# VectorE and ScalarE work through a block of linear attention in another order

## What is computed

```python
x = x + linear_attention(layernorm(x))     # x: 4 sequences, 2048 tokens, 256 features; 16 heads of 16
x = x + moe(layernorm(x))                  # 8192 tokens, 8 experts of 512, 2 for each token

# linear_attention: q = elu(x@Wq+bq)+1, k = elu(x@Wk+bk)+1, v = x@Wv+bv; per head and token i:
s = s + outer(k_i, v_i);  z = z + k_i
y_i = (q_i @ s) / (q_i @ z + 1e-6)         # then y @ Wo + bo

# moe: router logits, the two best experts, softmax over the two
out_t = sum over the two experts e of prob_e * (gelu(x_t@w1[e].T+b1[e]) @ w2[e].T + b2[e])
```

## Time and profile before

| | us |
|---|---|
| median of 3 runs (lowest, highest) | 1023.68 (1023.34, 1023.85) |
| the profiled execution, its own time | 1024.11 |
| its span in the trace | 1022.3 |
| PE busy | 917.8 (90%) |
| DVE busy | 754.4 (74%) |
| ACT busy | 681.3 (67%) |
| POOL busy | 621.1 (61%) |

### The profile page before, as it was taken

How to read it: one execution, slowest core, us unless ns; L and a number is a source line. 1 busy time by engine, 2 the same in 40 slices (tenths; PEclk the granted TensorE clock), 3 DMA queues, 4 the chain that set the end, 5 groups by cost and what they waited for, 6 DMA issues and landing times. The chain is left out here.

```text
span 1022.3 us, 33747 instructions
## 1 busy us (share of the span) xinstructions
PE 917.8 (90%) x10786; PEld 745.5 (73%) x10787; DVE 754.4 (74%) x2281; ACT 681.3 (67%) x1296; POOL 621.1 (61%) x564
## 2 busy tenths in 40 slices
PE   6799899899989999999987659899999999999995
PEld 3577677767777677767766338678999999999994
DVE  6689788988888888888887556456666666666663
ACT  8778888888878988888875315445555555555552
POOL 2135776777677767786673644447655565656565
PEclk9999999999999999999999769999999999999998
DMA  7626744554555354644441743435655656555554
GB/s 195 199 79 204 244 129 150 153 175 125 152 150 176 125 154 142 186 132 144 141 150 47 279 137 70 68 61 96 93 97 89 98 89 98 89 98 88 95 91 51
DMA packets 102584, 131.32 MB, mean 128 GB/s; under 512 B 15056, under 2 KB 89296, under 8 KB 101648
## 3 DMA queue, kind: packets, MB, share of 16 engines
q1 hardware_dynamic: 74336, 92.54, 32.2%
q0 software_dynamic: 25680, 35.01, 18.7%
q10 hardware_dynamic: 2464, 2.38, 0.7%
HBM read 64.29 MB, written 65.60 MB: 127 GB/s over the span
## 5 line engine op out<-in xcount | busy, mean ns | idle before, releaser
L1906 POOL DMA_INDIRECT out<-yt,to_token x135 | 216.7, 1605 | 176.6 <-DVE yt L1744 80.2
L1274 DVE SCALAR_TENSOR_TENSOR ahl<-pS,ahl 128x512 f16<-128x512 f32 x240 | 161.2, 682 | 42.4 <-ACT ahl L984 38.4
L984 ACT ACTIVATE ahl<-pS 128x512 f16<-128x512 f32 x240 | 142.2, 599 | 49.5 <-PE pS L654 32.2
L1789 POOL DMA_INDIRECT expert_in<-xn,cur x128 | 131.6, 1028 | 30.2 <-issue 26.0
L1196 ACT ACTIVATE g<-pS,b1s 128x256 f32<-128x256 f32 (+1 forms) x140 | 57.3, 462 | 94.6 <-PE pS L564 94.6
L564 PE MATMUL pS<-gT,w1s 128*128 128x256 f16 (+1 forms) x840 | 97.3, 272 | 4.3 <-DVE gT L1703 3.5
L564 PE MATMUL pF<-w2s,ghl 128*128 x816 | 95.6, 273 | 2.4 <-issue 1.5
L1710 DVE TENSOR_TENSOR ghl<-g,ghl 128x1024 f16<-128x1024 f32 (+1 forms) x68 | 83.0, 1221 | 19.4 <-ACT ghl L1221 12.6
L564 PE MATMUL pU<-w2s,ghl 128*128 x804 | 94.2, 273 | 1.9 <-issue 1.5
L564 PE MATMUL pF<-xT,was 128*128 128x512 f16 x384 | 92.8, 379 | 3.0 <-DVE xT L1279 2.9
L1783 POOL TENSOR_TENSOR state<-state,ut 128x272 f32<-128x272 f32 x64 | 49.9, 780 | 73.4 <-DVE ut L1314 72.5
(11 more groups left out here) (226 smaller groups left out, 2170.2 us busy)
## 6 DMA issues: line engine op xcount, KB each, us to landing
xg<-expert_in SPq DMA_DIRECT2D x64, 260.0 KB
qk_parts<-qkhl SPq DMA_DIRECT2D x64, 256.0 KB, 2.1
qst<-qk_parts SPq DMA_DIRECT2D x192, 64.0 KB
kst<-qk_parts SPq DMA_DIRECT2D x96, 128.0 KB
xs<-x SPq DMA_DIRECT2D x16, 512.0 KB
out<-x SPq DMA_DIRECT2D x16, 512.0 KB
w1raw<-w SPq DMA_DIRECT2D x16, 256.0 KB
w2raw<-w SPq DMA_DIRECT2D x4, 1024.0 KB, 7.2
```

Of the source, the lines that this page charges most:

```text
L984: nc.scalar.activation(ahl[:, b % 2, 0, n * 4 * C:(n + 1) * 4 * C], score_bank(fr, n)[:], ACT.Relu).then_inc(sc_hi, 1)
L1274: V.scalar_tensor_tensor(ahl[:, b % 2, 1, cols], score_bank(fr, n)[:], 0.0, ahl[:, b % 2, 0, cols], ALU.max, ALU.subtract).then_inc(sc_lo, 1)
L1789: G.indirect_dma_start(xg_dram, bass.IndirectOffsetOnAxis(ap=cur[:, qp, 2 * b + t:2 * b + t + 1], axis=0), xn2[:, qp, b], None).then_inc(s ...
L1906: G.indirect_dma_start(out, bass.IndirectOffsetOnAxis(ap=to_token[:, c % 2, s:s + 1], axis=0), yt[:, c % 2, s], None, compute_op=ALU.add). ...
```

## The change

Nothing is computed differently. VectorE's `router` is cut in two: `router_logits` (two instructions) stays where it was, the rest (maxima, indices, counts) moves behind `attention(3)`, `state_part(3)` and `logit_part(2)`. `norm2_shift` moves from ahead of `attention(0)` to behind `score_lo(1, 2)`; `out_lo(0)` comes ahead of the first statistics; `attention(1)` comes ahead of `residual(0)`; `score_lo(2, 3)` comes ahead of `norm1_shift` and `w1_low`. On ScalarE, `score_hi(2, 0)` comes ahead of `qk_high(2)` and `norm2_apply(0)`, and `out_hi(1)` and `score_hi(2, 2)` ahead of `norm2_apply(1)`. TensorE keeps its order and gets one wait: `out_transpose(s, 1)` also waits until `residual(s, 0)` has written x1.

```diff
--- before.py
+++ after.py
@@ -691,6 +691,8 @@
                     if g:
 
                         pe.wait_ge(lga_done, g)
+                        if b == 1:
+                            pe.wait_ge(x1_done, g)
                     for k in range(KC):
                         mm = nc.tensor.transpose(pA[:, k * C:(k + 1) * C], at[:, k * P:(k + 1) * P], ident)
                     mm.then_inc(aT_ps, 1)
@@ -1113,11 +1115,12 @@
                     score_hi(1, 3)
                 if fr:
                     feature(3)
+                if bk:
+                    score_hi(2, 0)
+                if fr:
                     qk_high(2)
                 if normed:
                     norm2_apply(0)
-                if bk:
-                    score_hi(2, 0)
                 if c == 0:
                     normalise(1, 0)
                 if fr:
@@ -1126,11 +1129,11 @@
                     score_hi(2, 1)
                 if fr and c >= 2:
                     w1_high()
+                if bk:
+                    out_hi(s, 1)
+                    score_hi(2, 2)
                 if normed:
                     norm2_apply(1)
-                if bk:
-                    out_hi(s, 1)
-                    score_hi(2, 2)
                 if normed:
                     norm2_apply(2)
                 if bk:
@@ -1361,7 +1364,7 @@
                     ins.then_inc(rt, 1)
                     dve.wait_ge(rt, RT * step + links[0])
 
-                def router():
+                def router_logits():
                     links[0] = 0
                     dve.wait_ge(lga_done, 4 * r + 4)
                     dve.wait_ge(ln2_rs, r + 1)
@@ -1372,6 +1375,8 @@
                     dve.wait_ge(lg_sum, r + 1)
                     link(r, V.scalar_tensor_tensor(lg[:], lga[:, rp], 1.0 / WS, rs2[:].unsqueeze(2).to_broadcast([P, B, E]),
                                                    ALU.mult, ALU.mult))
+
+                def router():
                     carry_wait(dve)
                     for b in range(B):
                         ins = V.max(mx[:, b], lg[:, b])
@@ -1508,8 +1513,6 @@
                     V.scalar_tensor_tensor(worh[:, 1], o, WS, worh[:, 0], ALU.mult, ALU.subtract).then_inc(wor_done, 1)
                 if c == STEPS:
                     row_data()
-                elif ro and c != STEPS + 1:
-                    norm2_shift()
                 if bk:
                     attention(0)
                     state_part(0)
@@ -1519,15 +1522,18 @@
                 ahead = nx or c == 1 and not front
                 if bk:
                     score_lo(1, 1)
+                    out_lo(s, 0)
                 if ahead:
                     norm1_stats(i + 1, 0, 2)
                 if c == STEPS + 1:
+                    router_logits()
                     router()
                     for b in range(B):
                         norm2_apply(b)
                 if bk:
-                    out_lo(s, 0)
                     score_lo(1, 2)
+                if ro and c not in (STEPS, STEPS + 1):
+                    norm2_shift()
                 if ahead:
                     norm1_stats(i + 1, 2, 3)
                 if bk:
@@ -1540,18 +1546,17 @@
                     norm2_shift()
                 if bk:
                     score_lo(2, 0)
+                    attention(1)
                     residual(s, 0)
-                    attention(1)
                     state_part(1)
                     score_lo(2, 1)
                     out_lo(s, 1)
                     score_lo(2, 2)
+                    score_lo(2, 3)
                 if ahead:
                     norm1_shift(i + 1)
                 if fr and c >= 2:
                     w1_low()
-                if bk:
-                    score_lo(2, 3)
                 if fr:
                     values(0)
                 if bk:
@@ -1569,11 +1574,13 @@
                 if c == STEPS + 1:
                     w2_low(0)
                 if ro and c != STEPS + 1:
-                    router()
+                    router_logits()
                 if bk:
                     attention(3)
                     state_part(3)
                     logit_part(s, 2)
+                if ro and c != STEPS + 1:
+                    router()
                 if c == 1 and not front:
                     w1_low()
```

More of the change, by code:

```diff
@@ L1128, in body @@
                     w1_high()
-                if normed:
-                    norm2_apply(1)
                 if bk:
@@ L1133, in body @@
                     score_hi(2, 2)
+                if normed:
+                    norm2_apply(1)
                 if normed:
```

## The result

| | before | changed |
|---|---|---|
| median of the runs, us | 1023.51 (1022.45 to 1023.85) | 1035.4 (1033.08 to 1039.34) |
| ratio, 95% interval | | 1.0122 [1.0104, 1.0141] |
| span of the profiled execution, us | 1022.3 | 1032.5 |
| busy PE, DVE, ACT, POOL in a steady block, us | | 31.00, 29.78, 28.09, 25.19 |

The change makes the kernel 1.2% slower; 1016.2 was predicted. The windows of the changed kernel show the steady block (205.40 to 239.75), one of the longer ones and the third block (c = 3, from 99.27 on); the columns are those of the earlier trace rows.

A forecast was written before the change was run, and what follows sets the result against it. The prediction saw a loop through PE, DVE and ACT, none full, as the bound. From 1024.11 it took 8.4 (0.6 a block, 14 blocks) and added 0.8 for the last iterations; against the median it predicted 1016.2, range 1009 to 1026.

The forecast's parts named there:

- norm2_shift: Replay step on VectorE behind `score_lo(1,2)`: the shift waits 0.2 for `low(1)`, and `score_lo(1,3)` starts at 283.34, against 283.35 before.
- the text's third case: Rival, 13%: `norm2_shift` also waits for `state_add(0)` behind `low(1)`, ending 0.77 later; period 33.7, time 1027.3.
- `w1_low` of c = 15: Earlier trace row: `w1_low` took 1.28, waiting for a scatter's end, yet got in ahead of the `state_add` that followed.
- the two port rivals: `w1_low` waiting for a scatter (25%, 1024.2 us), and `norm2_shift` losing the port for two GpSimd instructions (13%, 1027.3 us).
- the replay: One block replayed on paper in the new order with the trace's durations: period 32.97 instead of 33.56; 47%, 1011 to 1020.
- the rival: `w1_low` starts inside a GpSimd scatter and waits for its end: DVE loses 0.55 a block, time 1024.2; 25%.
- the new wait for x1: TensorE's `out_transpose(1)` waits for x1 of `residual(0)`: costs nothing, hidden by `values(0)`; without that cover 0.5.
- both new waits for ScalarE: New VectorE idle time ended by ScalarE: 0.8 ahead of `out_lo(0)` and 0.9 ahead of `score_lo(2,3)`.
- the lead of 1.45: `attention(0)` on VectorE goes 1.45 earlier, since `norm2_shift` with its 1.06 is gone from ahead of it.
- The last iterations: Block c = 16 and after: 1.1 gained at `score_hi(2,0)`, 1.9 lost by later router counts; together a loss of 0.8.
- the 5.61 of the earlier trace: Wait of `attention(3)` in c = 16, to 570.74; the router's rest now comes behind it, so counts come at about 573.9.

The follow-up runs named there:

- the swap: Changed kernel with GpSimd's first expert rows' scatter issued ahead of `state_add(0)` instead of behind it; 1015.99 us, ratio 0.9925, period 32.78.
- the four instructions: Changed kernel with `norm2_shift` at its new place as four instructions with one SBUF tensor input each; 1023.24 us, ratio 1.0034.
- w1 back: Changed kernel with `norm1_shift` and `w1_low` returned ahead of `score_lo(2, 3)`; 1015.34 us, ratio 0.996.
- the shift back: Changed kernel with `norm2_shift` alone returned to its old place ahead of `attention(0)`; 1007.68 us, ratio 0.9876.
- the shift early: Changed kernel with `norm2_shift` ahead of `score_lo(1, 0)`; 1004.31 us, ratio 0.9887. A second such kernel, with the c = 16 router uncut: 1013.59 us, 0.9906.
- the shift alone: Kernel before with only `norm2_shift` moved behind `score_lo(1, 2)`; 1026.13 us, ratio 1.0078.
- w1 late: Changed kernel with `w1_low` moved behind `score_lo(3, 1)`; 1021.52 us, ratio 1.0011.

## Why the prediction was wrong

**The step that failed is "*norm2_shift*": the shift "waits for its end, 282.9, a wait of 0.2".** It waited for the end of `low(1)` and the whole of `state_add(0)`, and took 0.94. This is the text's third case, held at 13% against `w1_low` of c = 15, which did get in ahead of a `state_add`. That row has a scatter in front of the `state_add`, not another tensor instruction; the swap shows that the neighbour decides. The forecast of that case, 1027.3, was still 8 short of the measured 1035.4, since it priced this wait alone.

**The second failure is that the two port rivals were priced one at a time, from the replay's phase.** Both came, and a third: the lost lead of the shift put L1262 0.69 into a scatter and `w1_low` onto `state_add(1)`, where the rival had it on the scatter. The sum closes against the kernel with the swap: 32.78 + 0.72 (`norm2_shift`, 0.94 - 0.22) + 0.60 (`w1_low`, 1.28 - 0.68) + 0.28 (L1262, 0.43 - 0.15) = 34.38, measured 34.35; so a gain of the swap by itself, apart from these waits, has hardly any room. Without `w1_low`'s part it gives 33.78 (33.72 measured), and for the four instructions 32.78 + 0.35 + 0.59 = 33.72 (33.64). In these kernels each wait lies on a stretch where VectorE has no slack, so each is paid in full. The sum doesn't fit every kernel: for w1 back it gives 32.78 + 0.72 = 33.50, measured 33.29, but there two instructions also stand elsewhere and fill idle time. 1.57 a block over the eleven steady blocks (c = 4 to 14) is 17; by the ratios, 0.9925 against 1.0122, the two kernels differ by 20.

**What was right.** The replay itself: its period of 32.97 had 0.2 for the shift's wait, and the kernels without further waits have 32.64 to 32.83. `out_transpose(3)` doesn't wait; `project(0)` comes 0.74 behind `x_lo`, as replayed; the new wait for x1 costs nothing; both new waits for ScalarE are there. But the lead of 1.45 that `attention(0)` was to get from the shift's departure is worth nothing: with the shift back the period is the same as with it early. `attention(0)` starts 9.49 behind `x_lo` with the shift early and 10.56 with it back, but `out_lo(0)` behind it starts at 12.45 in both: the gain is used up in waits for ScalarE.

**The last iterations** were charged with 0.8. From the last `x_lo` to the first activation of the experts the trace has 100.79 (617.78 - 516.99), before 101.93 (605.50 - 503.57): 1.1 less. The counts do come late, as said, in the changed kernel's rows:

```profile
585.11 0.21 PE L755 MATMUL pR<-cnt,chs 128*128 128x32 f16 x1 [6.50 <-DVE cnt L1395]
```

that is 68.12 behind the last `x_lo`, before 66.23. But `attention(3)` of c = 16, at 581.87, comes 64.88 behind it, before 67.17: 2.3 earlier. The reordered scores don't account for that. The products of `attend(3)` with v start 57.17 behind the last `x_lo` (574.16), before 58.88 (562.45): 1.7 earlier, where I had 1.1. VectorE starts `attention(3)` long after they are done, after a wait of 7.11, and the trace names no engine for it:

```profile
574.16 1.37 PE L675 MATMUL pO<-vhl,ahl 128*128 128x17 f16 x48 [0.69 <-DVE ahl L1277]
...
581.87 0.17 DVE L1301 TENSOR_SCALAR rden<-pO 128x16 f32<-128x16 f32 x1 [7.11 <-issue]
```

The changed kernel again, on another chip, waits 0.89 there and needs 95.71 to the experts. Of the fourteen traces eight, on two chips, have 94.0 to 96.2 for this stretch and the other six 100.6 to 102.9, with the changed kernel in both groups; the difference for the same kernel, 5.1, is far more than the 1.1. So a single pair of traces can't say what the change does to the last iterations, and the 5.61 of the earlier trace rows was a wait of this kind. What causes it is open.

**The sum, again.** From the first steady `x_lo` to the last (66.59 to 516.99) 450.40 us, before 436.95 (66.62 to 503.57): +13.45. Eleven blocks of some 0.85 make 9.4 of it; the third block gives 2.0 and one long block 1.9. From there to the end -3.2, of which 1.1 ahead of the experts (one trace each); the rest lies in the experts, where nothing was changed. In all +10.2, the difference of the spans.

**Still open.** The third block takes 37.45, before 35.47. The wait of `norm2_shift` isn't its cause: the shift takes 0.51 there in the changed kernel, and with w1 back, where it takes 0.15, the block still has 37.28. In all fourteen traces VectorE stands there for the load of x. Where it stands 0.85 or 1.59 the clock stays at 1.00 and the block takes 34.4 and 34.7 (both kernels with the shift early); in the other twelve it stands 1.75 to 3.35, and the block has a mean clock of 0.87 to 0.95 and takes 35.5 to 38.3. In the changed kernel the clock falls while TensorE has no work at all; its last product ended at 113.29:

```profile
111.27:114.00 2.73, 1.44 (x16) 0.82 (x14) 0.42 (x1) 2.73 (x7) 2.73 (x3) 1.00 1.01 282
114.00:116.00 2.00, 0.00 (x0) 0.00 (x0) 0.98 (x3) 0.43 (x1) 1.79 (x3) 0.68 0.38 139
116.00:118.00 2.00, 1.58 (x7) 1.33 (x8) 2.00 (x5) 0.62 (x2) 0.76 (x1) 0.50 0.40 132
118.00:120.00 2.00, 2.00 (x56) 1.95 (x54) 1.59 (x9) 1.50 (x3) 1.43 (x2) 0.50 0.58 158
120.00:122.00 2.00, 2.00 (x13) 1.45 (x12) 1.93 (x7) 1.00 (x2) 1.84 (x2) 0.62 0.74 235
122.00:124.00 2.00, 1.83 (x23) 1.34 (x22) 0.86 (x3) 1.25 (x4) 1.80 (x2) 1.00 0.24 81
```

It is at 0.50, the level of 1.2 GHz, for some 4 us behind that. What sets the length of the wait for x, and why single steady blocks lose the clock too, no run here tells.

## What to carry to other kernels

When VectorE instructions with two SBUF inputs are moved, look up what GpSimd runs at the new place and what it runs right behind that, and price all such waits together: the first shifts the phase at which the others meet GpSimd. Such a wait shows as a tiny instruction with a long duration, never as idle time, so read the groups by line and shape for means that have grown. Put such an instruction where its engine waits anyway, or leave a scatter behind the GpSimd instruction that it meets (the scatter held VectorE only in its later part here); rewriting it with one input removes its own wait but not those that the new phase makes.

## What the runs showed of the hardware

**GpSimd keeps the port from one tensor instruction to the next.** `norm2_shift` took 0.94 or 1.43 where `state_add` follows `low` at once, 0.22 with a scatter between. The Trainium skill, "SBUF — State Buffer", section "Who interferes with whom", says that whoever issues first gets the shared pair for the whole instruction; the traces agree, and add that a VectorE instruction that already waits can lose to the next one of GpSimd. Behind a scatter it did not: L1262 was done 0.08 behind the scatter's end, and `w1_low` of c = 15 ran ahead of a `state_add` that is 0.02 behind it.

**A scatter holds VectorE too, but not from its start.** I counted the two-input VectorE instructions of the two shifts, `w1_low` and `router_logits` that start inside a scatter, over all traces of this case from 60 to 560 us. Of 120 that start less than 0.3 us into it, none was stretched by more than 0.06. Of 39 between 0.3 and 0.4, 24 were, and of 38 between 0.6 and 0.7, 33; the short ones were then done 0.08 to 0.10 behind the scatter's end. The 21 that start later than 0.4 and were spared all stand beside scatters 0.98 or 0.99 long, where the usual one has 1.04; what distinguishes these is open. The prediction's argument that the port could be needed only at a scatter's start had it the wrong way round. The same section of the Trainium skill infers that descriptor generation needs the write interface, which a two-input tensor_tensor doesn't take; L1263 is one, and its 0.75 beside the scatter speaks against that.

**A longer block can be the clock's.** Nine single steady blocks in four traces (the changed kernel, the same again, w1 back, the shift alone) took 1.1 to 2.0 us more with the same program, and each has a mean granted clock of 0.95. In all four the shift is one instruction behind `score_lo(1,2)`; the kernel with w1 late has it there too and has no such block, so that isn't enough.
